# Three interleaved first groups instead of two, loaded and split in five parts, with eight warm-up matmuls instead of fourteen

## The chip, the cores and the metric

One NeuronCore of a Trainium2 chip runs the whole program. The metric is the device time of one execution in microseconds. TensorE (PE) multiplies, VectorE (DVE), ScalarE (ACT) and GpSimd (POOL) do elementwise work, and SyncE (SP) issues all the DMAs here. Each engine takes its own instructions in order; semaphores connect them.

## What is computed

x holds 64 sequences of 64 tokens with 1024 values each, so 4096 tokens. Four layers are applied one after another, each added to its input:

```python
x = x + _L0(x, lang, W, Wr, A, B)       # base x@W.T, plus top-2 gated low-rank experts (8 of rank 16)
x = x + _L1(x, cond, weights)           # a 64x64 matrix chosen per sequence, over the token axis
x = x + _L2(x, A[ids], B[ids])          # a rank-16 adapter chosen per sequence (64 adapters)
x = x + _L3(x, map, W, b, lA, lB)       # base x@W.T + b, plus a rank-16 adapter chosen per sequence (32)
```

## The kernel before, in words

All products are made in float32r with each operand split in a rounded high part and a low rest, in three passes (high x high, high x low, low x high). The split of a tile is an ACT instruction (the rounding, recorded at line 759) and then a DVE subtraction (line 1028).

**Weights first.** Up to about 300 us the kernel multiplies weights with weights, so that later every token tile needs fewer products: the matrices of the later layers are multiplied by (1 + W of layer 0), by the expert matrices and by the adapters. This is 61 groups. A group (list `GROUPS`, lines 56 to 58) is one stationary tile `stat` of 1024 x 128 (as 8 blocks of 128 x 128, 512 KB) times one chunk `mov` of 1024 x 512 (8 pieces of 128 x 512, 256 KB each): 8 steps k of 3 passes, so 24 matmuls of 512 columns into one PSUM bank (`product`, line 1390). The first nine groups share chunk 0 (`chunk_a`), the next nine chunk 1 (`chunk_b`).

**Stationary tiles** live in a ring of four slots (`RING`). `load_stat(g)` (line 379) waits until group g - 4 is done before it loads into that slot. For blocks of W of layer 0, POOL adds an identity to one block (line 655), which block depends on the group: blocks 4, 5 and 6 for groups 0, 1 and 2. Then ACT and DVE split the tile.

**The first groups.** Groups 0 and 1 run together (`TOGETHER`): for each k first the three passes of group 0, then of group 1 (lines 1397 to 1403), so that each piece of the chunk serves two groups as it arrives. Their tiles are loaded and split in two halves each, in the order half, piece 0, half, pieces 1 to 3, two halves, pieces 4 to 7 (lines 426 to 434 on SP, 822 to 830 on ACT, 1095 to 1103 on DVE). Tile 2 is loaded right behind, tile 3 at g = 0 of the loop.

**The loop over groups.** SP, ACT, DVE and POOL each run a loop over g of their own, written out by hand; its order is the order of each queue. In turn g, SP (lines 526 to 558) loads tile g + 3, then a piece of the next chunk, then 256 KB of `u3` rows (line 394), and stores the split u3 rows of the turn before (line 401), once they are split. ACT (lines 835 to 848) evicts group g - 1 (`group_hi`), rounds tile g + 2 (`stat_hi`), then a piece of the next chunk, then the u3 rows, which start at g = 1. DVE (lines 1133 to 1148) does the low parts in the same order. Before its loop DVE makes small setup tables (lines 1105 to 1127).

**Warm-up.** TensorE starts with 14 matmuls of the identity with itself (line 1385), which nobody reads.

**Token tiles.** From about 300 us on, 32 tiles of 128 tokens are processed in pairs. The change doesn't touch this.

Of the kernel before, what the change touches and what calls it, by code (L numbers as in the profile page):

```python
# [16 lines left out]
def build(nc, x, stat, mov, a0, wr, wc, u3, u2k, d3k, bias3, lang_ids, ids, out):  # L17
# [33 lines left out]

    TOGETHER, HALF_KB = 2, KB // 2
    M0_FIRST = M0_BLOCKS[HALF_KB:] + M0_BLOCKS[:HALF_KB]
# [31 lines left out]

    def halves(g, h):

        return h * TOGETHER + g + 1

# [65 lines left out]
    with ctx:  # L155
# [162 lines left out]
        def sem(name):  # L318
            return ctx.enter_context(nc.semaphore(name))

        ld_stat = [sem(f"ld_stat{n}") for n in range(RING)]
        ld_half = [[sem(f"ld_half{n}_{h}") for h in range(2)] for n in range(TOGETHER)]
        ld_mov = [[sem(f"ld_mov{n}_{k}") for k in range(KB)] for n in range(2)]
# [11 lines left out]
            sem, ("pool_const", "pool_stat", "pool_mov", "pool_md", "pool_mb", "pool_mix", "pool_s", "pool_ud"))  # L335
        act_half, act_stat, act_mov, act_u3, act_ev, act_hl, act_t = map(
            sem, ("act_half", "act_stat", "act_mov", "act_u3", "act_ev", "act_hl", "act_t"))
        act_x0, act_x1, act_s, act_part, act_ud, act_mix, act_exp = map(
            sem, ("act_x0", "act_x1", "act_s", "act_part", "act_ud", "act_mix", "act_exp"))
        act_h2, act_h2T, act_h3, act_h3T, act_hgT = map(sem, ("act_h2", "act_h2T", "act_h3", "act_h3T", "act_hgT"))  # L340
        act_yp, act_La, act_Lb, act_Ra, act_Rb = map(sem, ("act_yp", "act_La", "act_Lb", "act_Ra", "act_Rb"))
        dve_half, dve_stat, dve_mov, dve_u3, dve_ev, dve_hl, dve_set, dve_t1, dve_t4a, dve_t4, dve_t = map(
            sem, ("dve_half", "dve_stat", "dve_mov", "dve_u3", "dve_ev", "dve_hl", "dve_set", "dve_t1", "dve_t4a", "dve_t4",
                  "dve_t"))
# [31 lines left out]
        def _(sp):  # L376
# [44 lines left out]

            def load_half(g, h):
                own = slice(h * HALF_KB, (h + 1) * HALF_KB)
                sp.dma_start(sraw[g][:, own, :], stat[GROUPS[g][1]][:, own, :]).then_inc(ld_half[g][h], 16)

            load_half(0, 0)
            load_piece(0, 0)
            load_half(1, 0)
            for k in range(1, HALF_KB):
                load_piece(0, k)  # L430
            load_half(0, 1)
            load_half(1, 1)
            for k in range(HALF_KB, KB):
                load_piece(0, k)
            for g in range(TOGETHER, RING - 1):
# [199 lines left out]
        def _(pool):  # L635
# [11 lines left out]
            def stat_identity(g):  # L647
                s = GROUPS[g][1]
                if s in M0_BLOCKS:
                    raw = sraw[g % RING]  # L650
                    if g < TOGETHER:
                        pool.wait_ge(ld_half[g][s // HALF_KB], 16)
                    else:
                        pool.wait_ge(ld_stat[g % RING], 16 * slot_loads(g))
                    nc.gpsimd.tensor_tensor(out=raw[:, s, :], in0=raw[:, s, :], in1=ident[:, :], op=ALU.add).then_inc(pool_stat, 1)  # L655
# [101 lines left out]
        def _(act):  # L757
# [55 lines left out]

            def half_hi(g, h):
                own = slice(h * HALF_KB, (h + 1) * HALF_KB)
                if h == GROUPS[g][1] // HALF_KB:
                    act.wait_ge(pool_stat, stat_adds(g))
                else:
                    act.wait_ge(ld_half[g][h], 16)
                round_to(st[g][hi][:, own, :], sraw[g][:, own, :]).then_inc(act_half, 1)  # L820

            half_hi(0, 0)
            piece_hi(0, 0)
            half_hi(1, 0)
            for k in range(1, HALF_KB):
                piece_hi(0, k)
            half_hi(0, 1)
            half_hi(1, 1)
            for k in range(HALF_KB, KB):
                piece_hi(0, k)  # L830
            def x0_hi(j):
# [3 lines left out]
            for g in range(G):  # L835
                if g >= 1:
                    group_hi(g - 1)
                if g + 2 < G:
                    stat_hi(g + 2)
# [186 lines left out]
        def _(dve):  # L1026
# [62 lines left out]

            def half_lo(g, h):  # L1090
                own = slice(h * HALF_KB, (h + 1) * HALF_KB)
                dve.wait_ge(act_half, halves(g, h))
                rest(st[g][lo][:, own, :], sraw[g][:, own, :], st[g][hi][:, own, :]).then_inc(dve_half, 1)

            half_lo(0, 0)
            piece_lo(0, 0)
            half_lo(1, 0)
            for k in range(1, HALF_KB):
                piece_lo(0, k)
            half_lo(0, 1)  # L1100
            half_lo(1, 1)
            for k in range(HALF_KB, KB):
                piece_lo(0, k)

# [28 lines left out]
            for g in range(G):  # L1133
                if g >= 1:
                    group_lo(g - 1)
                if g + 2 < G:
                    stat_lo(g + 2)
# [246 lines left out]
        def _(pe):  # L1384
            WARM_UP = 14
            pe.wait_ge(pool_const, 2)
# [10 lines left out]
            for k in range(KB):  # L1397
                pe.wait_ge(dve_mov, k + 1)
                for g in range(TOGETHER):
                    pe.wait_ge(dve_half, halves(g, k // HALF_KB))  # L1400
                    last = product(g, k)
                    if k == KB - 1:
                        last.then_inc(pe_group, 1)
# [341 lines left out]
```

## Time and profile before

| | us |
|---|---|
| time, median of 3 runs | 910.5 (908.39 to 910.94) |
| profiled execution, device time | 909.23 |
| its span, first to last instruction | 907.5 |
| PE busy | 897.7 (99%) |
| DVE busy | 551.3 (61%) |
| ACT busy | 346.2 (38%) |
| POOL busy | 230.5 (25%) |
| DMA engines, mean busy share | 67% |

The span is what the profile covers; the device time of the same execution lies 1.7 us above it. A busy engine is one that is inside an instruction; a matmul's record covers its way through the array, so neighbours overlap and starts, not ends, tell the rate. Idle time of an engine that isn't the bottleneck costs nothing. The mean granted TensorE clock over the span is 0.998 of its full level.

### The profile page before, as it was taken

How to read it: one execution, taken by the hardware profiler on the slowest of the kernel's cores; microseconds unless marked ns; L12 is line 12 of the kernel's file. 1: busy time of each engine (PE TensorE's matmuls, PEld its weight loads, DVE VectorE, ACT ScalarE, POOL GpSimd, SP SyncE). 2: the span in 40 equal slices, each digit the busy share in tenths (PEclk: the TensorE clock that was granted, in tenths of full speed). 3: DMA queues.
4: the chain of work that ended last, by engine and by line, in shares of the span. 5: the costliest groups of instructions: out<-in, count | busy, mean ns of one | idle time of the engine just before them, and what ended most of it. 6: DMA issues, size and time to landing. Idle time of an engine off the chain costs nothing.

```text
span 907.5 us, 14863 instructions
## 1 busy us (share of the span) xinstructions
PE 897.7 (99%) x4788; PEld 798.2 (88%) x4788; DVE 551.3 (61%) x1421; ACT 346.2 (38%) x800; POOL 230.5 (25%) x349
## 2 busy tenths in 40 slices
PE   8999999999999999999999999999999999999997
PEld 7888888888888888999998998998998999999997
DVE  6554444354367426568567667577676576676675
ACT  5543343333334323333434433434434334334333
POOL 1010010011010003522523424414415325225230
PEclk9999999999999999999999999999999999999999
DMA  6878686999663563666756756766666567657664
GB/s 249 299 256 289 208 251 206 307 341 262 188 198 117 176 198 129 191 180 181 218 181 182 219 181 186 204 198 194 184 198 216 168 183 218 187 178 217 188 200 148
DMA packets 105602, 187.69 MB, mean 207 GB/s; under 512 B 15926, under 2 KB 66870, under 8 KB 105526
## 3 DMA queue, kind: packets, MB, share of 16 engines
q1 hardware_dynamic: 105526, 186.76, 66.9%
q8 instruction: 38, 0.62, 0.3%
q14 instruction: 38, 0.31, 0.1%
HBM read 143.20 MB, written 49.81 MB: 213 GB/s over the span
## 4 chain that ended last, share of the span: by engine, by line
PE 90%; SPq 4%; DMA 3%; issue 1%; POOL 1%; ACT 1%; DVE 0%; DVEq 0%; POOLq 0%
PE ps_o L1393 27%; PE ps_d L1419 16%; PE ps_w L1427 13%; PE ps_d L1427 9%; PE ps_s L1393 9%; PE ps_o L1440 5%; PE ps_d L1434 4%; PE ps_o L1451 3%; SPq L443 1%; PE ps_s L1457 1%; DMA mdraw<-t 1%; SPq L471 1%; PE ps_w L1434 1%; DMA mixraw<-wc 1%; DMA chunk_a_raw<-mov 1%
## 5 line engine op out<-in xcount | busy, mean ns | idle before, releaser
L1028 DVE TENSOR_TENSOR stat_lo<-stat_raw,stat_hi 128x1024 fp32r<-128x1024 f32 (+1 forms) x127 | 140.6, 1108 | 22.9 <-ACT stat_hi L759 20.4
L759 ACT ACTIVATE stat_hi<-stat_raw 128x1024 fp32r<-128x1024 f32 (+1 forms) x127 | 116.8, 932 | 17.1 <-POOL stat_raw L655 6.5
L1419 PE MATMUL ps_d<-w_hi,stat_hi 128*128 128x512 f32 x256 | 105.9, 414 | 0.8 <-POOL w_lo L680 0.8
L1419 PE MATMUL ps_d<-w_lo,stat_hi 128*128 128x512 f32 x256 | 101.1, 395 | 0.0
L1419 PE MATMUL ps_d<-w_hi,stat_lo 128*128 128x512 f32 x256 | 100.8, 394 | 0.0
L1393 PE MATMUL ps_o<-chunk_a_hi,stat_hi 128*128 128x512 f32 x216 | 84.5, 391 | 0.8 <-DVE chunk_a_lo L1028 0.7
L1393 PE MATMUL ps_o<-chunk_a_hi,stat_lo 128*128 128x512 f32 x216 | 84.1, 389 | 0.0
L1393 PE MATMUL ps_o<-chunk_a_lo,stat_hi 128*128 128x512 f32 x216 | 84.0, 389 | 0.0
L680 POOL CAST w_hi<-mdraw 128x512 fp32r<-128x512 f32 x32 | 20.0, 624 | 219.8 <-DMA mdraw<-t 219.8
L655 POOL TENSOR_TENSOR stat_raw<-stat_raw,ident 128x128 f32<-128x128 f32 x40 | 22.5, 562 | 184.9 <-DMA stat_raw<-stat 184.9
L1393 PE MATMUL ps_o<-chunk_b_hi,stat_hi 128*128 128x512 f32 x152 | 59.1, 389 | 0.0
L1393 PE MATMUL ps_o<-chunk_b_hi,stat_lo 128*128 128x512 f32 x152 | 59.1, 389 | 0.0
L1393 PE MATMUL ps_o<-chunk_b_lo,stat_hi 128*128 128x512 f32 x152 | 59.1, 389 | 0.0
L1419 PEld LDWEIGHTS ps_d<-w_hi,stat_hi 128*128 128x128 f32 x256 | 48.5, 190 | 10.8 <-issue 0.9
L1419 PEld LDWEIGHTS ps_d<-w_lo,stat_hi 128*128 128x128 f32 x256 | 48.1, 188 | 11.2
L1419 PEld LDWEIGHTS ps_d<-w_hi,stat_lo 128*128 128x128 f32 x256 | 48.4, 189 | 8.2
L759 ACT ACTIVATE y_hi<-y_raw 128x356 fp32r<-128x356 f32 x48 | 24.0, 499 | 66.9 <-DVE y_raw L1274 47.8
L1393 PEld LDWEIGHTS ps_o<-chunk_a_hi,stat_hi 128*128 128x128 f32 x216 | 40.5, 188 | 10.2 <-DVE chunk_a_lo L1028 1.4
L1245 DVE TENSOR_TENSOR outb<-ps_o,bias_row 128x356 f32<-128x356 f32 (+1 forms) x93 | 41.9, 506 | 10.7 <-PE ps_o L1451 10.3
L1393 PEld LDWEIGHTS ps_o<-chunk_a_lo,stat_hi 128*128 128x128 f32 x216 | 40.6, 188 | 8.4
L1393 PEld LDWEIGHTS ps_o<-chunk_a_hi,stat_lo 128*128 128x128 f32 x216 | 40.6, 188 | 8.3
L709 POOL TENSOR_TENSOR stat_raw<-stat_raw 128x512 f32<-128x512 f32 x32 | 44.5, 1390 | 12.7 <-DMA stat_raw<-x 11.1
(223 smaller groups left out, 2269.5 us busy)
## 6 DMA issues: line engine op xcount, KB each, us to landing
up<-tu SPq DMA_DIRECT2D x124, 256.0 KB, 4.2
stat_raw<-stat SPq DMA_DIRECT2D x59, 512.0 KB, 4.2
mdraw<-t SPq DMA_DIRECT2D x128, 208.0 KB, 2.9
stat_raw<-x SPq DMA_DIRECT2D x32, 512.0 KB, 3.5
out<-outb SPq DMA_DIRECT2D x30, 512.0 KB, 5.5
t<-md_a SPq DMA_DIRECT2D x16, 576.0 KB, 6.1
rows_raw<-x SPq DMA_DIRECT2D x32, 256.0 KB, 3.4
chunk_a_raw<-mov SPq DMA_DIRECT2D x24, 256.0 KB, 5.2
```

The source lines that it names most:

```text
L655: nc.gpsimd.tensor_tensor(out=raw[:, s, :], in0=raw[:, s, :], in1=ident[:, :], op=ALU.add).then_inc(pool_stat, 1)
L680: last = nc.gpsimd.tensor_copy(w[part][:, :, MD_AT:P_AT].rearrange("p k (q r) -> p k q r", r=RANK), rows.rearrange("p q (k r) -> p k q r", ...
L709: nc.gpsimd.tensor_tensor(out=dst, in0=in0, in1=in1, op=op).then_inc(pool_s, 1)
L759: return nc.scalar.activation(dst, src, ACT.Copy)
L1028: return nc.vector.tensor_tensor(out=dst, in0=src, in1=rounded.bitcast(F32), op=ALU.subtract)
L1245: nc.vector.tensor_tensor(out=dst[:, OX[n]], in0=out_bank(turn, n)[:, OK[n]], in1=bias_row[:, OX[n]], op=ALU.add).then_inc(dve_out[n], 1)
L1393: last = nc.tensor.matmul(ps_g[g % BANKS][:, :], st[g % RING][a][:, k, :], mchunk[c % 2][v][:, k, :], start=k == 0 and m == 0, stop=k == K ...
L1419: last = nc.tensor.matmul(plain_bank(t)[:, 0:WCOLS], rows[a][:, k, :], w[c][:, k, :], start=k == 0 and m == 0, stop=k == KB - 1 and m == l ...
L1427: last = nc.tensor.matmul(ps[:, 0:SH], rows[a][:, k, :], weights[c][:, k, :], start=first and k == 0 and m == 0, stop=k == HALF_KB - 1 and ...
L1434: last = nc.tensor.matmul(ps, hgT[t % 2][a][:, :], b03[c][:, cols], start=first and m == 0, stop=m == len(PASSES) - 1, skip_group_check=True)
L1440: last = nc.tensor.matmul(out_bank(turn, n)[:, 0:OW[n]], mix[turn % 2][a][:, :], y[t % 2][c][:, Y[n]], start=first and m == 0, stop=m == l ...
L1451: return nc.tensor.matmul(out_bank(turn, n)[:, OK[n]], stackT[:, :], up[:, OX[n]], start=first, stop=True, skip_group_check=True)
```

## The change

The first three groups run together instead of two. Their tiles are no longer loaded and split in two halves of four blocks, but in five parts of 1, 1, 2, 2 and 2 blocks. For each part SP loads the part of all three tiles, then the pieces of the chunk with the same k. One semaphore a part (`ld_part[q]`) counts all three tiles' loads, and whoever uses any of them waits for all three. ACT and DVE take tile 0's part, the first piece, the parts of tiles 1 and 2, and then the second piece, if there is one. Tile 3 is loaded in the loop's first turn, as before, and its split stands right behind the parts, on DVE ahead of the setup tables. Warm-up has 8 matmuls. The diff, without the renamed semaphores:

```diff
@@ -49,7 +49,8 @@
     M0_BLOCKS, B0_BLOCK, U2_BLOCKS = list(range(KB)), KB, list(range(KB + 1, 2 * KB + 1))
     D_CHUNKS, M3_CHUNKS = (0, 1, 2), (3, 4)
 
-    TOGETHER, HALF_KB = 2, KB // 2
+    TOGETHER, HALF_KB = 3, KB // 2
+    PARTS = (range(0, 1), range(1, 2), range(2, 4), range(4, 6), range(6, 8))
     M0_FIRST = M0_BLOCKS[HALF_KB:] + M0_BLOCKS[:HALF_KB]
 
     M0_BY_TWO = [s + h for s in range(HALF_KB) for h in (0, HALF_KB)]
@@ -83,9 +84,12 @@
 
         return g // RING + (1 if g % RING >= TOGETHER else 0)
 
-    def halves(g, h):
-
-        return h * TOGETHER + g + 1
+    def parts(g, q):
+
+        return q * TOGETHER + g + 1
+
+    def part_of(k):
+        return [k in ks for ks in PARTS].index(True)
 
     def piece(c, k):
         return c * KB + k
...
@@ -419,19 +423,15 @@
                 sp.dma_start(table[first:first + OWN, :, RAW_AT:FULL].bitcast(F32),
                              source[first:first + OWN].rearrange("a p k r -> a p (k r)")).then_inc(st_own, 16)
 
-            def load_half(g, h):
-                own = slice(h * HALF_KB, (h + 1) * HALF_KB)
-                sp.dma_start(sraw[g][:, own, :], stat[GROUPS[g][1]][:, own, :]).then_inc(ld_half[g][h], 16)
-
-            load_half(0, 0)
-            load_piece(0, 0)
-            load_half(1, 0)
-            for k in range(1, HALF_KB):
-                load_piece(0, k)
-            load_half(0, 1)
-            load_half(1, 1)
-            for k in range(HALF_KB, KB):
-                load_piece(0, k)
+            def load_part(g, q):
+                own = slice(PARTS[q].start, PARTS[q].stop)
+                sp.dma_start(sraw[g][:, own, :], stat[GROUPS[g][1]][:, own, :]).then_inc(ld_part[q], 16)
+
+            for q, ks in enumerate(PARTS):
+                for g in range(TOGETHER):
+                    load_part(g, q)
+                for k in ks:
+                    load_piece(0, k)
             for g in range(TOGETHER, RING - 1):
                 load_stat(g)
             sp.dma_start(lang_sb[:, :], lang_ids[None, :].to_broadcast([P, TILES * BT])).then_inc(ld_lang, 16)
@@ -649,7 +649,7 @@
                 if s in M0_BLOCKS:
                     raw = sraw[g % RING]
                     if g < TOGETHER:
-                        pool.wait_ge(ld_half[g][s // HALF_KB], 16)
+                        pool.wait_ge(ld_part[part_of(s)], 16 * TOGETHER)
                     else:
                         pool.wait_ge(ld_stat[g % RING], 16 * slot_loads(g))
                     nc.gpsimd.tensor_tensor(out=raw[:, s, :], in0=raw[:, s, :], in1=ident[:, :], op=ALU.add).then_inc(pool_stat, 1)
@@ -811,23 +811,23 @@
                     last = round_to(both[hi][:, n, :], raw[:, n, :])
                 last.then_inc(act_t, 1)
 
-            def half_hi(g, h):
-                own = slice(h * HALF_KB, (h + 1) * HALF_KB)
-                if h == GROUPS[g][1] // HALF_KB:
+            def part_hi(g, q):
+                own = slice(PARTS[q].start, PARTS[q].stop)
+                if GROUPS[g][1] in PARTS[q]:
                     act.wait_ge(pool_stat, stat_adds(g))
                 else:
-                    act.wait_ge(ld_half[g][h], 16)
-                round_to(st[g][hi][:, own, :], sraw[g][:, own, :]).then_inc(act_half, 1)
-
-            half_hi(0, 0)
-            piece_hi(0, 0)
-            half_hi(1, 0)
-            for k in range(1, HALF_KB):
-                piece_hi(0, k)
-            half_hi(0, 1)
-            half_hi(1, 1)
-            for k in range(HALF_KB, KB):
-                piece_hi(0, k)
+                    act.wait_ge(ld_part[q], 16 * TOGETHER)
+                round_to(st[g][hi][:, own, :], sraw[g][:, own, :]).then_inc(act_part0, 1)
+
+            for q, ks in enumerate(PARTS):
+                part_hi(0, q)
+                piece_hi(0, ks[0])
+                for g in range(1, TOGETHER):
+                    part_hi(g, q)
+                for k in ks[1:]:
+                    piece_hi(0, k)
+            stat_hi(TOGETHER)
+
             def x0_hi(j):
                 act.wait_ge(ld_x0, 16 * (j + 1))
                 round_to(x0[hi][:, :, :], x0raw[:, :, :]).then_inc(act_x0, 1)
@@ -835,7 +835,7 @@
             for g in range(G):
                 if g >= 1:
                     group_hi(g - 1)
-                if g + 2 < G:
+                if TOGETHER < g + 2 < G:
                     stat_hi(g + 2)
                 for c, k in pieces_at(g):
                     piece_hi(c, k)
@@ -1087,20 +1087,19 @@
                     last = rest(both[lo][:, n, :], raw[:, n, :], both[hi][:, n, :])
                 last.then_inc(dve_t, 1)
 
-            def half_lo(g, h):
-                own = slice(h * HALF_KB, (h + 1) * HALF_KB)
-                dve.wait_ge(act_half, halves(g, h))
-                rest(st[g][lo][:, own, :], sraw[g][:, own, :], st[g][hi][:, own, :]).then_inc(dve_half, 1)
-
-            half_lo(0, 0)
-            piece_lo(0, 0)
-            half_lo(1, 0)
-            for k in range(1, HALF_KB):
-                piece_lo(0, k)
-            half_lo(0, 1)
-            half_lo(1, 1)
-            for k in range(HALF_KB, KB):
-                piece_lo(0, k)
+            def part_lo(g, q):
+                own = slice(PARTS[q].start, PARTS[q].stop)
+                dve.wait_ge(act_part0, parts(g, q))
+                rest(st[g][lo][:, own, :], sraw[g][:, own, :], st[g][hi][:, own, :]).then_inc(dve_part0, 1)
+
+            for q, ks in enumerate(PARTS):
+                part_lo(0, q)
+                piece_lo(0, ks[0])
+                for g in range(1, TOGETHER):
+                    part_lo(g, q)
+                for k in ks[1:]:
+                    piece_lo(0, k)
+            stat_lo(TOGETHER)
 
             dve.wait_ge(ld_lang, 16)
             dve.wait_ge(pool_const, CONSTS)
@@ -1133,7 +1132,7 @@
             for g in range(G):
                 if g >= 1:
                     group_lo(g - 1)
-                if g + 2 < G:
+                if TOGETHER < g + 2 < G:
                     stat_lo(g + 2)
                 for c, k in pieces_at(g):
                     piece_lo(c, k)
@@ -1382,7 +1381,7 @@
 
         @block.tensor
         def _(pe):
-            WARM_UP = 14
+            WARM_UP = 8
             pe.wait_ge(pool_const, 2)
             for _ in range(WARM_UP):
                 nc.tensor.matmul(ps_w[:, 0:P], ident[:, :], ident[:, :], start=True, stop=True)
@@ -1397,7 +1396,7 @@
             for k in range(KB):
                 pe.wait_ge(dve_mov, k + 1)
                 for g in range(TOGETHER):
-                    pe.wait_ge(dve_half, halves(g, k // HALF_KB))
+                    pe.wait_ge(dve_part0, parts(g, part_of(k)))
                     last = product(g, k)
                     if k == KB - 1:
                         last.then_inc(pe_group, 1)
```

## Rows read from the trace of the kernel before

**Rows 1.** The page: busy us of each engine, share of the span.
```profile
PE 897.7 (99%) x4788; PEld 798.2 (88%) x4788; DVE 551.3 (61%) x1421; ACT 346.2 (38%) x800; POOL 230.5 (25%) x349
```

**Rows 2.** Stretches: length; busy us of PE, PEld, DVE, ACT, POOL; clock, DMA, GB/s.
```profile
0.00:20.00 20.00, 17.72 (x78) 14.88 (x79) 11.95 (x25) 11.02 (x17) 3.61 (x14) 1.00 0.67 241
```

**Rows 3.** Waits up to 80 us: engine, line <- releaser: us, times, longest.
```profile
PEld ps_o L1393 <- DVE chunk_a_lo L1028: 1.4, 2, 1.2
```

**Rows 4.** Timeline to 7.3 us: start, us, engine, line, what [idle before].
```profile
0.75 0.40 SPq L424 DMA_DIRECT2D stat_raw<-stat  x1
1.21 0.42 SPq L388 DMA_DIRECT2D chunk_a_raw<-mov  x1
1.53 5.93 PE L1388 MATMUL ps_w<-ident 128*128 128x128 f32 x28 [1.53 <-POOL ident L638]
...
4.44 0.63 ACT L759 ACTIVATE chunk_a_hi<-chunk_a_raw 128x512 fp32r<-128x512 f32 x1
...
5.75 0.69 DVE L1028 TENSOR_TENSOR stat_lo<-stat_raw,stat_hi 128x512 fp32r<-128x512 f32 x1
7.22 0.47 PE L1393 MATMUL ps_o<-chunk_a_hi,stat_hi 128*128 128x512 f32 x1
```

**Rows 5.** Timeline, 8 to 20 us: the chunk's pieces and group 2.
```profile
8.16 1.89 ACT L759 ACTIVATE chunk_a_hi<-chunk_a_raw 128x512 fp32r<-128x512 f32 x3 [2.44 <-DMA chunk_a_raw<-mov]
...
9.57 0.50 PE L1393 MATMUL ps_o<-chunk_a_hi,stat_hi 128*128 128x512 f32 x1 [0.72 <-DVE chunk_a_lo L1028]
...
18.24 1.22 DVE L1028 TENSOR_TENSOR stat_lo<-stat_raw,stat_hi 128x1024 fp32r<-128x1024 f32 x1
...
19.52 0.50 PE L1393 MATMUL ps_o<-chunk_a_hi,stat_hi 128*128 128x512 f32 x1
```

**Rows 6.** Timeline of TensorE: first matmuls of group 3 and of group 4.
```profile
25.13 0.39 PE L1393 MATMUL ps_s<-chunk_a_hi,stat_hi 128*128 128x512 f32 x1
...
30.57 0.39 PE L1393 MATMUL ps_o<-chunk_a_hi,stat_hi 128*128 128x512 f32 x1
```

**Rows 7.** L1388 alone: one stretch; grouped by form, 5.5:6.2 and 6.9:7.2 us.
```profile
1.53:6.88 5.35, 5.35 (x25) 5.35 (x26) 1.00 0.77 242
...
L1388 PE MATMUL ps_w<-ident 128*128 128x128 f32 x6 | 1.5, 421 | 0.0
...
L1388 PE MATMUL ps_w<-ident 128*128 128x128 f32 x5 | 0.9, 310 | 0.0
```

**Rows 8.** Groups by line and form, whole span: a 128x128 tile on DVE.
```profile
L1176 DVE TENSOR_TENSOR hg<-ps_d,gates 128x128 f32<-128x128 f32 x32 | 9.3, 291 | 1.1
```

**Rows 9.** Table of stretches, 4 to 12 us, columns as in rows 2.
```profile
4.00:8.00 4.00, 4.00 (x23) 3.88 (x22) 2.01 (x3) 1.66 (x3) 0.00 (x0) 1.00 0.74 240
8.00:12.00 4.00, 3.28 (x15) 2.38 (x14) 2.16 (x4) 2.74 (x5) 1.33 (x2) 1.00 1.05 407
```

**Rows 10.** Timeline: group 0's last matmul, SP's load into slot 0, first u3 rows.
```profile
18.42 0.39 PE L1393 MATMUL ps_o<-chunk_a_lo,stat_hi 128*128 128x512 f32 x1
...
18.84 0.33 SPq L383 DMA_DIRECT2D stat_raw<-stat  x1
...
19.68 0.43 SPq L394 DMA_DIRECT2D rows_raw<-u  x1
```

**Rows 11.** Timeline, 22 to 29 us: what happens to tile 4.
```profile
22.41 0.46 POOL L655 TENSOR_TENSOR stat_raw<-stat_raw,ident 128x128 f32<-128x128 f32 x1 [5.11 <-DMA stat_raw<-stat]
...
25.46 0.63 ACT L759 ACTIVATE rows_hi<-rows_raw 128x512 fp32r<-128x512 f32 x1 [4.55 <-DMA rows_raw<-u]
...
26.48 1.05 ACT L759 ACTIVATE stat_hi<-stat_raw 128x1024 fp32r<-128x1024 f32 x1
...
27.56 1.23 DVE L1028 TENSOR_TENSOR stat_lo<-stat_raw,stat_hi 128x1024 fp32r<-128x1024 f32 x1
```

**Rows 12.** The u3 loads (L394), all eight: time from issue to landing.
```profile
DMA to landing us min/median/max: 3.4/3.7/6.8
```

**Rows 13.** Timeline of DVE: low part of tile 5.
```profile
30.51 1.22 DVE L1028 TENSOR_TENSOR stat_lo<-stat_raw,stat_hi 128x1024 fp32r<-128x1024 f32 x1
```

More of the change, by code:

```diff
@@ L321, in build @@
         ld_stat = [sem(f"ld_stat{n}") for n in range(RING)]
-        ld_half = [[sem(f"ld_half{n}_{h}") for h in range(2)] for n in range(TOGETHER)]
+        ld_part = [sem(f"ld_part{q}") for q in range(len(PARTS))]
         ld_mov = [[sem(f"ld_mov{n}_{k}") for k in range(KB)] for n in range(2)]
@@ L335, in build @@
             sem, ("pool_const", "pool_stat", "pool_mov", "pool_md", "pool_mb", "pool_mix", "pool_s", "pool_ud"))
-        act_half, act_stat, act_mov, act_u3, act_ev, act_hl, act_t = map(
-            sem, ("act_half", "act_stat", "act_mov", "act_u3", "act_ev", "act_hl", "act_t"))
+        act_part0, act_stat, act_mov, act_u3, act_ev, act_hl, act_t = map(
+            sem, ("act_part0", "act_stat", "act_mov", "act_u3", "act_ev", "act_hl", "act_t"))
         act_x0, act_x1, act_s, act_part, act_ud, act_mix, act_exp = map(
@@ L341, in build @@
         act_yp, act_La, act_Lb, act_Ra, act_Rb = map(sem, ("act_yp", "act_La", "act_Lb", "act_Ra", "act_Rb"))
-        dve_half, dve_stat, dve_mov, dve_u3, dve_ev, dve_hl, dve_set, dve_t1, dve_t4a, dve_t4, dve_t = map(
-            sem, ("dve_half", "dve_stat", "dve_mov", "dve_u3", "dve_ev", "dve_hl", "dve_set", "dve_t1", "dve_t4a", "dve_t4",
+        dve_part0, dve_stat, dve_mov, dve_u3, dve_ev, dve_hl, dve_set, dve_t1, dve_t4a, dve_t4, dve_t = map(
+            sem, ("dve_part0", "dve_stat", "dve_mov", "dve_u3", "dve_ev", "dve_hl", "dve_set", "dve_t1", "dve_t4a", "dve_t4",
                   "dve_t"))
```

## The prediction

> **What bounds the kernel now.** The page first: TensorE is busy 897.7 us, 99% of the span [rows 1], so only what makes TensorE wait can move the time, and the change touches it only in the first groups. The table of stretches says how much there is to win: of the first 20 us TensorE was busy 17.72 [rows 2]. So about 2.3 us of idle time, 1.53 of it before the first warm-up matmul, plus whatever the warm-up matmuls themselves cover. The waits name most of the rest: the weight loads of TensorE stood 1.4 us behind pieces of the moving chunk [rows 3]. The timeline gives the places. Warm-up runs from 1.53, the first real matmul starts at 7.22, although its operands were split by about 6.4 (the last entry of DVE is 5.75 + 0.69): here warm-up itself is late [rows 4]. After six matmuls TensorE idles until 9.57, because piece 1 landed only at 8.16, and group 2 starts at 19.52 behind a split that DVE began at 18.24, after its setup work [rows 5]. Group 3 starts at 25.13 and group 4 at 30.57; these are 24 matmuls or 5.44 us apart, so 0.2267 us a matmul, without a gap [rows 6].
>
> **Part 1, warm-up.** TensorE made 25 records in the 5.35 us from 1.53 to 6.88, 0.214 us each [rows 7]; a warm-up matmul leaves two (28 for 14). Eight make 16 x 0.214 = 3.4 us and end near 5.0. The clock matters: in the last stretch before the first real matmul the same instruction shortened from 421 ns to a mean of 310 ns [rows 7], so TensorE went from its lower level (1.2 GHz) to its upper (2.4 GHz) near 6.9, after 5.35 us of unbroken work. After the change it works 3.4 us, pauses until the first operands are there, and goes on. Either the rise comes as early as now (cost nothing) or, at the worst the rows allow, after another 5.35 us of unbroken work. No row decides.
>
> The Trainium skill, page "TensorE: Matmul & The Clock Gate", Part 1, says that the engine begins throttled and that activity releases it. The trace agrees in kind; what a pause in warm-up does no row here shows.
>
> **Part 2, the loads.** Now four halves and eight pieces, 12 loads of 256 KB. After: 15 parts (six of 64 KB, nine of 128 KB) and eight pieces, 23 loads, 3.5 MB instead of 3 MB. SP starts one each 0.46 us [rows 4]. Piece 0 moves from second to fourth, its issue from 1.21 to 0.75 + 3 x 0.46 = 2.13. It now lands 3.2 us after its issue at the latest (ACT takes it at 4.44) [rows 4]; I take 3.1, so 5.2. Then 0.63 on ACT and 0.69 on DVE [rows 4] make 6.55, and the first matmul starts at 6.6, not 7.22. The small parts cost 0.29 us each on DVE [rows 8], and not more on ACT, which was the shorter of the two at 512 columns; they fit between. Nine matmuls take 2.04 us, to 8.65. Piece 1 is the eighth load, issued at 3.97, with 896 KB up to and with it. Bounds for its landing: 3.97 + 3.2 = 7.2 and the 8.13 of now (1024 KB) [rows 5]. I take 7.7, since the same slow stretch of 4 to 8 us (240 GB/s) lies across it [rows 9]; with ACT and DVE it is ready at 9.1, a stall of 0.45. From then a step of 448 KB is wanted each 2.04 us, 220 GB/s, while 407 arrived from 8 to 12 us [rows 9], and DVE needs 0.69 + 3 x 0.29 = 1.6 us a step: no further stall. The three identity adds on POOL (0.5 us) lie ahead of steps 4 to 7, some 2 us before they are needed. Group 2's late split disappears too, as it is now part of these. Seven steps: 9.1 + 14.3 = 23.4 is where group 3 can start, against 25.13: a gain of 1.75 us. Tile 3's load moves back behind 11 more issues on SP, to about 14 us, and has 9 us to land and be split; nothing.
>
> With the clock at its lower level until 6.6 + 5.35 = 11.95, matmuls come each 0.43 us: 12.5 of 72 by then, the other 59.5 take 13.5, and group 3 starts at 25.4. I take half of this 2.0 us, since the pause is short beside the work around it: 24.4.
>
> The Trainium skill, page "DMA: Bandwidth & Descriptors", section Bandwidth, speaks against this part: it wants transfers batched to 1 MiB and gives a 64 KB one 138 GB/s. By that rate, an estimate, the six small loads (393 KB) would take 2.8 us of the engines, and the time would be some 1.5 us higher than mine. The rows have no load of such a size in this stretch.
>
> **Part 3, what comes free later.** This is the edit's other side. The ring has four slots; group 4's tile goes into slot 0, and SP waits for group 0's end to load it. Now group 0's last matmul is the 45th of 48; SP issues at 18.84, and its companions follow: a piece, then u3 rows at 19.68 [rows 10]. What follows is a chain in which ACT's order counts: group 0's eviction, then the u3 rows (landed 25.46), group 1's eviction, and only then tile 4 at 26.48, although it had landed by 22.41; DVE splits it from 27.56 to 28.79 [rows 11]. So from SP's issue to "tile 4 ready" it takes 9.95 us, and group 4 starts at 30.57 [rows 6]: a slack of only 1.8 us. With three groups interleaved, group 0's last matmul is the 66th of 72. It starts 7 x 0.2267 = 1.59 before group 3, and SP issues 0.42 after (now 18.42 and 18.84 [rows 10]). With 24.4 that is 23.2, 4.4 us later than now. Queued behind SP's wait are a piece of chunk b, the u3 rows and group 5's tile, as now, so the chain moves as a block. Its length is bounded from below by the rows landing in the median 3.7 us instead of 5.8 (7.9 us in all) and from above by their longest, 6.8 (11.0) [rows 12]. I take 9.3, nearer to the one measured in the same burst of loads. Group 4 then starts at 32.5 instead of 24.4 + 5.44 = 29.8: TensorE stalls 2.7 us, and against 30.57 the kernel is 1.95 us later. Tile 5 was ready at 31.73 [rows 13], 12.9 after SP's issue, so 36.1, and is wanted at 32.5 + 5.44 = 37.9; tile 6 follows a whole group later with its load. The delay of group 4 passes unchanged to the end, as TensorE is saturated there.
>
> **Sum.** Group 3 starts now 16.3 us of matmuls and 1.6 of stalls after 7.22. After: start -0.6, stalls 0.45 for 1.6 -1.15, clock +1.0, so 0.75 earlier; then the stall in front of group 4, +2.7; net +1.95. The profiled execution took 909.23 us with a span of 907.5, so 911.2 for it; it lies 1.3 under the median of 910.5, which gives 912.4.
>
> **Rivals.** (a) The change does what it seems to be for: the clock rises in time and the u3 rows land in 3.7 us. Group 3 at 23.4, SP at 22.2, tile 4 at 30.1, so 0.5 us earlier than now; with tile 4 earlier still, TensorE's own 23.4 + 5.44 = 28.85 and 1.7 us. 908.8 to 910.0. For it: at least half of the eight loads of u3 rows landed within 3.7 us [rows 12]. Against: the one that counts took 5.8, in a burst of six loads after an idle stretch, as it will again. Chance 0.22. (b) Slower: the clock. The pause between warm-up and work keeps TensorE at the lower level to about 12 us. Group 3 at 25.4, SP at 24.2, tile 4 at 34.2: +3.6, 914.1. It decides once the rise comes later than about 10 us. For it: the unbroken 5.35 us of now. Chance 0.2. (c) Small loads are slow, so that piece 1 lands 1.5 us later; everything follows, +3.4, 913.9. Chance 0.08. The forecast itself, tile 4's chain with the clock somewhere between, has 0.5, and its own range is +0.7 to +2.7: 911.2 to 913.2.
>
> **Chances.** About 0.3%, or 2.7 us, is what a measurement can tell from no change. Faster by more than that wants (a) beyond its end and a lucky spread of runs: 0.08. Slower by more is (b), and the larger part of (c): 0.24. Within: 0.68. The range takes in (a)'s upper part and (b): 909.0 to 914.3.
>
> **What would show it.** Right: SP's load into slot 0 near 22 to 23.5, TensorE idle in front of group 4 for 2 to 3 us with DVE's split of tile 4 as what ended it, group 3 starting before 25. Wrong: group 4 starting before 30.57, u3 rows landing in under 4 us, no idle time in front of group 4. The clock's step: L1393 matmuls 0.43 us apart after 6.9. Should a second stall stand before group 5 or 6, or group 3 start late because of tile 3, the sum is short of a term.

## The result, and the profile after

The changed kernel took 912.52 us (median of 22 runs), the kernel before 910.56 us beside it: a ratio of 1.0029, 95% interval 1.0016 to 1.0042. The medians lie 2.0 us apart, the means (913.43 and 910.69) 2.7, since the changed kernel has some long executions, up to 919.61. By the ratio it is slower by 1.5 to 3.8 us, about 2.6 us, just under the 0.3% that the prediction named as what can be told from no change. The forecast was 912.4.

The page of the changed kernel, first line of busy times, answers to [rows 1]. Then TensorE's waits, which name what is new, and the stretches (length, then busy us of PE, PEld, DVE, ACT, POOL, then clock, DMA share, GB/s).

```profile
PE 897.3 (99%) x4776; PEld 797.6 (88%) x4776; DVE 548.3 (60%) x1431; ACT 348.3 (38%) x810; POOL 232.5 (26%) x349
```
```profile
PE ps_o L1450 <- ACT h2T L759: 2.5, 3, 1.9
PE ps_o L1392 <- DVE stat_lo L1028: 2.2, 1, 2.2
PE ps_w L1387 <- POOL ident L638: 1.5, 1, 1.5
PE ps_o L1392 <- DVE chunk_a_lo L1028: 1.1, 1, 1.1
```
```profile
0.00:40.00 40.00, 35.19 (x146) 29.02 (x146) 22.34 (x47) 19.90 (x39) 5.11 (x17) 1.00 0.74 242
40.00:300.00 260.00, 260.00 (x1149) 215.29 (x1148) 131.64 (x182) 100.42 (x162) 26.16 (x48) 1.00 0.78 241
```

TensorE has as much work as before, fewer by the twelve warm-up records. A wait of 2.2 us behind `stat_lo` is new. From 40 to 300 us nothing waits, and the same 1149 matmul records stand there before and after, so all that the weight part loses is lost in the first 40.

The timeline of its start, start time first, then duration (answers to [rows 4] and [rows 5]):

```profile
1.53 3.78 PE L1387 MATMUL ps_w<-ident 128*128 128x128 f32 x16 [1.53 <-POOL ident L638]
...
2.14 0.43 SPq L392 DMA_DIRECT2D chunk_a_raw<-mov  x1
...
6.36 0.80 PE L1392 MATMUL ps_o<-chunk_a_hi,stat_hi 128*128 128x512 f32 x1 [1.05 <-DVE chunk_a_lo L1028]
...
7.38 0.63 PE L1392 MATMUL ps_o<-chunk_a_lo,stat_hi 128*128 128x512 f32 x1
...
7.61 0.63 ACT L759 ACTIVATE chunk_a_hi<-chunk_a_raw 128x512 fp32r<-128x512 f32 x1 [0.39 <-DMA chunk_a_raw<-mov]
7.81 0.63 PE L1392 MATMUL ps_o<-chunk_a_hi,stat_hi 128*128 128x512 f32 x1
...
10.25 0.39 PE L1392 MATMUL ps_o<-chunk_a_hi,stat_hi 128*128 128x512 f32 x1
```

Warm-up is over early, and the first real matmul starts at 6.36 instead of 7.22. But it has a record of 0.80 us, and the seven behind it stand 0.43 us apart and last 0.63 us, not 0.39: TensorE was at 1.2 GHz until 10.1, where its clock record says that it rose. The chain that ended last shows the rest, start and length:

```profile
6.36 17.01 PE ps_o L1392 x66
23.37 0.02 issue
23.39 0.33 SPq L387
...
24.23 4.63 DMA rows_raw<-u
28.86 0.02 issue
28.89 0.64 ACT rows_hi L759
29.52 0.49 ACT md_a L759
30.01 0.95 ACT stat_hi L759
30.96 0.02 issue
30.98 1.36 DVE stat_lo L1028
32.34 0.04 issue
32.38 16.62 PE ps_o L1392 x72
```

This is the chain of the forecast, link by link: 66 matmuls to group 0's end, SP's load into slot 0 (which lets the u3 rows behind it go), the u3 rows' landing, their rounding, an eviction, tile 4's rounding, its low part, group 4. Tile 4 itself had been there before: POOL began its addition at 27.44, 2.6 us before ACT took the tile up at 30.01. Group 3 starts at 24.55 (before 25.13), group 4 at 32.38 (before 30.57 [rows 6]).

```profile
24.55 0.39 PE L1392 MATMUL ps_s<-chunk_a_hi,stat_hi 128*128 128x512 f32 x1
...
27.44 0.46 POOL L655 TENSOR_TENSOR stat_raw<-stat_raw,ident 128x128 f32<-128x128 f32 x1 [8.24 <-DMA stat_raw<-stat]
```

So 0.6 us won at group 3 became 1.8 us lost at group 4.

### The profile page after: what moved, and what is told of

Its sections match the earlier page's. It is cut to its first block, busy times and chain, and to the rows that moved or that the text cites. A ratio compares the mean times of both kernels' runs of the same rounds, so it can differ in the third digit from the quotient of the medians.

```text
span 910.2 us, 14869 instructions
## 1 busy us (share of the span) xinstructions
PE 897.3 (99%) x4776; PEld 797.6 (88%) x4776; DVE 548.3 (60%) x1431; ACT 348.3 (38%) x810; POOL 232.5 (26%) x349
## 4 chain that ended last, share of the span: by engine, by line
PE 89%; DMA 3%; SPq 3%; issue 1%; POOL 1%; ACT 1%; DVE 1%; DVEq 0%; POOLq 0%
PE ps_o L1392 27%; PE ps_d L1418 17%; PE ps_w L1426 12%; PE ps_d L1426 9%; PE ps_s L1392 8%; PE ps_o L1439 4%; PE ps_d L1433 4%; PE ps_o L1450 3%; DMA mdraw<-t 2%; PE ps_s L1456 1%; SPq L443 1%; PE ps_w L1433 1%; DMA stat_raw<-x 1%; SPq L456 1%; DMA rows_raw<-u 1%
## 5 line engine op out<-in xcount | busy, mean ns | idle before, releaser
L1028 DVE TENSOR_TENSOR stat_lo<-stat_raw,stat_hi 128x1024 fp32r<-128x1024 f32 (+3 forms) x137 | 143.6, 1051 | 28.0 <-ACT stat_hi L759 25.5
L759 ACT ACTIVATE stat_hi<-stat_raw 128x1024 fp32r<-128x1024 f32 (+3 forms) x137 | 118.5, 880 | 22.4 <-POOL stat_raw L655 8.9
```

Source lines behind the costliest of these rows:

```text
L759: return nc.scalar.activation(dst, src, ACT.Copy)
L1028: return nc.vector.tensor_tensor(out=dst, in0=src, in1=rounded.bitcast(F32), op=ALU.subtract)
```

## Experiments

Two theories stood against each other for the main loss. The first: ACT takes the u3 rows ahead of tile 4, and with slot 0 free 4.5 us later this wait ends last. The rival: slot 0 is simply free too late, whatever ACT does. A second question was what the short warm-up does to TensorE's clock. In these profiled executions I read four points: when TensorE's clock rose (from the granted clock, which agrees with the length of the matmuls), when groups 3 and 4 started, and the time from SP's load into slot 0 to tile 4's low part done (the chain). The single executions of a kernel scatter over several us (those of the kernel before, beside the changed one, from 907.85 to 913.54), so that the times need their intervals, and one profiled execution stands for itself only. Ratios are to the kernel before in the same batch, since that kernel's own median moved from 908.5 to 910.7 us between batches.

### 14 warm-up matmuls in the changed kernel

```diff
-            WARM_UP = 8
+            WARM_UP = 14
```

> The changed kernel with 14 warm-up matmuls instead of 8, all else as changed. Theory (the pause after a short warm-up delays TensorE's clock): the clock rises near 7 us instead of 10.1, no L1392 matmul stands 0.43 us from the next, group 3 starts near 23.6 instead of 24.55, SP loads slot 0 near 22.4, group 4 starts near 31.4 instead of 32.4; the time is about 1.0 us under that of the changed kernel and about 1 us over the kernel before. Rival (the clock rises when it does, whatever warm-up does, and the later start of real work at 7.2 costs what it saved): group 3 at 24.5 or later, group 4 at 32.4 or later, no gain.

Measured: 912.86 us beside 908.51 of the kernel before, ratio 1.0052 (1.0031 to 1.0073). The clock rose at 6.3, and group 3 started at 23.80, 0.75 us earlier: so far the theory. SP loaded slot 0 at 22.64. But the u3 rows landed only at 29.5, and group 4 started at 32.89, after a longer stall:

```profile
29.52 0.63 ACT L759 ACTIVATE rows_hi<-rows_raw 128x512 fp32r<-128x512 f32 x1 [5.75 <-DMA rows_raw<-u]
...
31.61 1.23 DVE L1028 TENSOR_TENSOR stat_lo<-stat_raw,stat_hi 128x1024 fp32r<-128x1024 f32 x1
...
32.89 0.50 PE L1392 MATMUL ps_o<-chunk_a_hi,stat_hi 128*128 128x512 f32 x1 [3.48 <-DVE stat_lo L1028]
```

And something that I had not foreseen. The stretches behind the stall (clock is the third number from the end):

```profile
25.00:33.60 8.60, 5.12 (x23) 3.94 (x22) 4.06 (x7) 3.82 (x7) 0.92 (x2) 1.00 0.78 257
33.60:37.00 3.40, 3.40 (x10) 2.63 (x9) 2.77 (x4) 1.34 (x2) 0.46 (x1) 0.50 0.95 321
37.00:40.00 3.00, 3.00 (x14) 2.47 (x14) 1.42 (x3) 2.23 (x4) 0.00 (x0) 1.00 1.02 365
```

The granted clock fell to one half at 33.6 and came back at 37.0. The (x10) counts every matmul that touches the stretch; TensorE started 8 in these 3.4 us, 0.43 us apart, where it starts 15 at 0.2267, so that the fall cost some 7 x 0.2267 = 1.6 us on top of the stall's 3.5. SP's load was 0.75 us earlier, but the chain behind it took 10.2 us instead of 8.9, since the rows landed in 6.0 us and not in 4.7; the head start went into a longer stall. That the time would fall with group 3 is not borne out: 1.0 us less than the changed kernel was expected, and by the ratios it is 2.1 us more.

### The u3 rows two turns later in the changed kernel

```diff
-    U3_FIRST, U3_UNITS = 1, 2 * NE3 * RANK // P
+    U3_FIRST, U3_UNITS = 3, 2 * NE3 * RANK // P
```

> The changed kernel with the u3 rows loaded and split from turn 3 on instead of turn 1, so that ACT does not stand behind their landing before it rounds tiles 4 and 5. Theory (the stall before group 4 is ACT's order: u3 rows ahead of tile 4): tile 4 is rounded as soon as it has landed, some 4 us after SP's issue, and is ready 6.9 us after the issue instead of 8.9; group 4 starts near 30.3 instead of 32.4, and the time falls 2.1 us, to that of the kernel before or slightly under. Rival (slot 0 free too late: the load itself and the two splits make the stall): tile 4's load lands no earlier, group 4 starts at 32 or later, the time stays. Second rival: the rows come in the way of a later tile (a stall in front of group 6 to 8), so that the time is given back.

Measured: 908.16 us, ratio to the kernel before 0.9995 (0.9979 to 1.0011), where the changed kernel has 1.0029. Nothing waits in front of group 4, which starts at 29.90, its 24 matmuls after group 3 at 24.46. SP's load went out at 23.29, no earlier than in the changed kernel, and the chain took 6.2 us, not 8.9:

```profile
26.64 0.46 POOL L655 TENSOR_TENSOR stat_raw<-stat_raw,ident 128x128 f32<-128x128 f32 x1 [7.53 <-DMA stat_raw<-stat]
27.13 1.06 ACT L759 ACTIVATE stat_hi<-stat_raw 128x1024 fp32r<-128x1024 f32 x1 [2.23 <-POOL stat_raw L655]
...
28.23 1.22 DVE L1028 TENSOR_TENSOR stat_lo<-stat_raw,stat_hi 128x1024 fp32r<-128x1024 f32 x1 [2.06 <-ACT stat_hi L759]
```

The stall is gone with slot 0 free as late as ever, so the rival falls. No later tile stalled. By the ratios the gain over the changed kernel is 3.1 us, more than the 2.1 expected; the section on the hardware has what may be the rest.

### Two groups together in five parts, 8 warm-up matmuls

```diff
-    TOGETHER, HALF_KB = 3, KB // 2
+    TOGETHER, HALF_KB = 2, KB // 2
```

> The changed kernel with two groups together instead of three, still in five parts and with 8 warm-up matmuls. Theory (the third interleaved group is what delays slot 0): group 0 ends near 19, SP loads slot 0 near 19, tile 4 is ready near 28.5 to 29 and nothing stalls in front of group 4; group 3 starts at 24.5 to 25.0, group 4 at 30 to 30.5; the time is 1.5 to 2.4 us under the changed kernel, so from equal to 0.6 us under the kernel before. Rival (parts and short warm-up are what costs): group 4 starts at 31.5 or later even so.

Measured: 909.82 us, ratio 1.0014 (0.9997 to 1.0030). Slot 0 was loaded at 18.68, tile 4 ready at 28.9, group 3 started at 24.61 and group 4 at 30.05 without a stall, although the clock rose only at 10.7:

```profile
18.68 0.33 SPq L387 DMA_DIRECT2D stat_raw<-stat  x1
...
27.67 1.22 DVE L1028 TENSOR_TENSOR stat_lo<-stat_raw,stat_hi 128x1024 fp32r<-128x1024 f32 x1
...
30.05 0.39 PE L1392 MATMUL ps_o<-chunk_a_hi,stat_hi 128*128 128x512 f32 x1
```

The third group is what turned the slack of 1.8 us into a stall; the five parts don't. The time missed its range (from equal to 0.6 us under the kernel before): the median lies 1.3 us over it, and its interval overlaps that of the changed kernel, so that it is the trace that tells the two apart here, not the time. The third group with the old halves was not run.

### 8 warm-up matmuls in the kernel before

```diff
-            WARM_UP = 14
+            WARM_UP = 8
```

> The kernel before with 8 warm-up matmuls instead of 14. Theory (a pause in TensorE's work delays its clock): first real matmul near 6.5 instead of 7.2, clock rising near 10 instead of 6.9; its six matmuls take 2.6 us instead of 1.4 and piece 1 is late anyway, so little is lost at first; group 2 starts 0 to 0.6 us later than 19.5, group 4 0 to 0.6 us later than 30.6, time +0 to +0.6. Rival (the clock does not care): group 2 at 19.5 as now, time equal, clock at 6.9.

Measured: 908.36 us, ratio 0.9997 (0.9978 to 1.0015), so no difference that can be measured. The one profiled execution is the extreme of all: first matmul at 5.91, but the clock at its lower level until 13.95, 4 us later than expected, and groups 3 and 4 at 26.60 and 32.04, 1.5 us behind the kernel before.

```profile
5.91 0.79 PE L1393 MATMUL ps_o<-chunk_a_hi,stat_hi 128*128 128x512 f32 x1 [0.59 <-DVE chunk_a_lo L1028]
...
9.37 0.80 PE L1393 MATMUL ps_o<-chunk_a_hi,stat_hi 128*128 128x512 f32 x1 [0.54 <-DVE chunk_a_lo L1028]
...
13.38 0.63 PE L1393 MATMUL ps_o<-chunk_a_hi,stat_hi 128*128 128x512 f32 x1
...
14.33 0.39 PE L1393 MATMUL ps_o<-chunk_a_hi,stat_hi 128*128 128x512 f32 x1
```

TensorE paused twice here, 0.6 us before the first matmul and 0.5 us before the seventh. The expected range for group 4 was missed by 0.9 us, since I had taken 10 us as the latest rise. The median doesn't move with it, and the profiled execution (910.45 us) lies 2.1 us over the median, so other executions probably had an earlier rise. That this kernel has one is not shown; the split order below, with 8 warm-up matmuls too, shows two.

### 14 warm-up matmuls and late u3 rows

```diff
-            WARM_UP = 8
+            WARM_UP = 14
-    U3_FIRST, U3_UNITS = 1, 2 * NE3 * RANK // P
+    U3_FIRST, U3_UNITS = 3, 2 * NE3 * RANK // P
```

> The changed kernel with 14 warm-up matmuls and with the u3 rows from turn 3 on. Theory (two separate costs, the late clock and the u3 rows ahead of tile 4 on ACT): clock up near 6.3 to 6.9, group 3 near 23.8 as with 14 warm-up matmuls alone, tile 4 ready some 7 us after SP's issue at 22.6, so group 4 starts near 29.3 to 29.6 and TensorE idles under 0.6 us in front of it; the clock does not fall. Time 0.4 to 0.9 us under the kernel with late u3 rows and 8 warm-up matmuls, 1 us under the kernel before. Rival (warm-up length does nothing for the sum): group 4 starts at 29.9 or later, as with 8.

Measured: 910.81 us, ratio 1.0015 (0.9998 to 1.0032). The expected gain did not come. The clock rose at 6.8 and never fell, and nothing stalled in front of group 4, but group 3 started only at 24.40 and group 4 at 29.84, as with 8. The full clock ran TensorE into the pieces, at 12.0, as its waits show:

```profile
PE ps_o L1392 <- DVE chunk_a_lo L1028: 0.5, 1, 0.5
```

So what the rival said of the sum holds here: 14 warm-up matmuls brought group 4 nothing, and the ratio is 0.0020 (1.8 us) over that of late u3 rows with 8, where 0.4 to 0.9 us less was expected.

### The u3 rows split one turn later

SP loads them as in the changed kernel; only the order of ACT and DVE changes.

```diff
-                for u in u3_at(g):
+                for u in u3_at(g - 1):
                     u3_hi(u)
...
-                for u in u3_at(g):
+                for u in u3_at(g - 1):
                     u3_lo(u)
```

> The changed kernel with the u3 rows loaded by SP exactly where they are, but split by ACT and DVE one turn later, behind tile 4's split. It tells ACT's order from the transfer itself. Theory (the order on ACT): tile 4 is rounded as soon as it has landed and POOL has added, near 27.5 to 28.5, is ready near 30.3, and group 4 starts near 30.3 instead of 32.4; time 2 us under the changed kernel. Rival (the u3 load takes bandwidth from tile 4 and the late u3 case gained from its absence): tile 4 lands 4 us or more after SP's issue and group 4 starts at 31.5 or later, or a later tile stalls because SP stands in front of the rows' store.

Measured: 908.44 us, ratio 0.9983 (0.9967 to 1.0000). SP's load at 23.89, tile 4 rounded as soon as it was there, ahead of the u3 rows:

```profile
27.45 0.46 POOL L655 TENSOR_TENSOR stat_raw<-stat_raw,ident 128x128 f32<-128x128 f32 x1 [7.79 <-DMA stat_raw<-stat]
27.94 1.06 ACT L759 ACTIVATE stat_hi<-stat_raw 128x1024 fp32r<-128x1024 f32 x1 [2.44 <-POOL stat_raw L655]
...
29.86 0.63 ACT L759 ACTIVATE rows_hi<-rows_raw 128x512 fp32r<-128x512 f32 x1 [0.34 <-DMA rows_raw<-u]
```

The u3 rows took 5.1 us to land (24.74 to 29.86) and held up nobody. The chain took 6.4 us, and group 4 followed group 3 (25.06) without a gap, at 30.50. It is the order on ACT, not the transfer. By the ratios the time is 4.2 us under the changed kernel, twice the 2 us expected. In this execution the clock rose early, at 4.5, inside warm-up; the first real matmul at 6.55 was fast at once, and TensorE then waited 1.0 us at 12.6 for a piece. The early clock bought nothing either.

### Two groups in five parts, 14 warm-up matmuls

```diff
-    TOGETHER, HALF_KB = 3, KB // 2
+    TOGETHER, HALF_KB = 2, KB // 2
-            WARM_UP = 8
+            WARM_UP = 14
```

> The changed kernel with two groups together and 14 warm-up matmuls: the five parts alone are left of the change. Theory: the clock is up by 6.9, the first real matmul starts at 7.2, step 1 is ready at 8.2 to 8.9, group 3 starts at 23.9 to 24.4 and group 4 at 29.3 to 29.9 without a stall (slot 0 free near 18.3, tile 4 ready near 28.3); time 0.7 to 1.2 us under the kernel before. Rival (the parts cost as much as they bring): group 4 starts at 30.5 or later.

Measured: 909.99 us, ratio 1.0005 (0.9986 to 1.0024). Clock at 7.3, group 3 at 24.70, group 4 at 30.14, no stall: 0.4 us ahead of the kernel before at group 4, where 0.7 to 1.3 was expected, and not to be seen in the time. Parts alone bring little.

### Late u3 rows in the kernel before

```diff
-    U3_FIRST, U3_UNITS = 1, 2 * NE3 * RANK // P
+    U3_FIRST, U3_UNITS = 3, 2 * NE3 * RANK // P
```

> The kernel before with the u3 rows from turn 3 on: the control for the late u3 rows. Theory: there is no stall before group 4 to remove (1.8 us of slack), so group 4 starts at 30.6 as before and the time is the same within what can be measured; tile 4 is ready 2 us earlier, near 26.8. Rival (late u3 rows help anywhere, by less traffic early): group 3 or 4 starts over 0.5 us earlier, time 0.5 us or more lower.

Measured: 909.28 us, ratio 0.9992 (0.9978 to 1.0006). DVE began tile 4's low part at 24.22 instead of 27.56, and group 4 started at 30.29, 0.3 us earlier, as group 3 did. Tile 4 was ready 5 us before it was needed, and it brought nothing: with slack there is nothing to win from the order. This is the control for late u3 rows and for the split order.

### The changed kernel again, beside the split order

> The changed kernel itself once more, beside the two below on the same chip. Theory: tile 4 stands behind the u3 rows on ACT, so group 4 starts 8.9 to 10.3 us after SP's load into slot 0, with a stall of 2 to 3.5 us in front of it, and the time is 2 to 3 us over the kernel before. The clock rises anywhere from 4.5 to 14 us, since with 8 warm-up matmuls it has risen at 4.5, 10.0, 10.1, 10.7 and 14.0. Rival: the stall seen in one execution was its own, and this one shows none.

Measured: 913.26 us, ratio 1.0030 (1.0011 to 1.0049), a stall of 3.1 us in front of group 4 at 33.21. The clock rose at 9.9 and fell behind this stall too:

```profile
33.21 0.50 PE L1392 MATMUL ps_o<-chunk_a_hi,stat_hi 128*128 128x512 f32 x1 [3.06 <-DVE stat_lo L1028]
...
33.80:37.20 3.40, 3.40 (x10) 2.66 (x9) 2.90 (x4) 1.25 (x2) 0.45 (x1) 0.50 0.90 304
37.20:40.00 2.80, 2.80 (x14) 2.27 (x13) 1.14 (x2) 1.81 (x3) 0.00 (x0) 1.00 1.04 363
```

The split order again, same edit as above:

> The changed kernel with the u3 rows split one turn later, again, beside the changed kernel. Theory: no stall in front of group 4, ready 6.4 to 7 us after SP's load; time 2 to 3 us under the changed kernel and 1 to 1.5 us under the kernel before. Rival: the lead over the kernel before was chance; then it is within 0.5 us of it.

Measured: 909.54 us, ratio 0.9987 (0.9971 to 1.0003); so 3.7 us under the changed kernel, more than the stall and than the 2 to 3 us expected, and 1.1 us under the kernel before, a lead that its interval doesn't tell from nothing. The chain took 6.9 us, group 4 started at 29.85 with a wait of 0.2 us, the clock had risen at 5.1.

And with 14 warm-up matmuls:

```diff
-            WARM_UP = 8
+            WARM_UP = 14
```

> The changed kernel with the u3 rows split one turn later and 14 warm-up matmuls. Theory: the clock rises by 7.3 at the latest, first real matmul at 7.0 to 7.4, group 3 at 23.6 to 24.4, group 4 at 29.1 to 29.9, no stall; time equal to the 8 warm-up case within 0.7 us, since an early rise there buys back a late one. Rival (the clock is the larger cost): 1 us or more under the 8 warm-up case.

Measured: 910.25 us, ratio 0.9988 (0.9967 to 1.0009). Clock at 6.5, group 3 at 24.52, group 4 at 30.23, both 0.1 to 0.3 us later than the latest expected. The time is that with 8 within 0.7 us, as the theory said.

All profiled executions together, in us; the chain runs from SP's load into slot 0 to tile 4's low part done:

| kernel | clock up | group 3 | chain | stall | group 4 | ratio to before |
|---|---|---|---|---|---|---|
| before | 6.9 | 25.13 | 9.95 | none | 30.57 | 1 |
| before, 8 warm-up | 14.0 | 26.60 | 11.1 | none | 32.04 | 0.9997 |
| before, u3 rows late | 7.2 | 24.85 | 6.9 | none | 30.29 | 0.9992 |
| two groups in parts | 10.7 | 24.61 | 10.2 | none | 30.05 | 1.0014 |
| two groups in parts, 14 | 7.3 | 24.70 | 9.5 | none | 30.14 | 1.0005 |
| changed | 10.1 | 24.55 | 8.9 | 2.2 | 32.38 | 1.0029 |
| changed, again | 9.9 | 24.55 | 9.8 | 3.1 | 33.21 | 1.0030 |
| changed, 14 | 6.3 | 23.80 | 10.2 | 3.5 | 32.89 | 1.0052 |
| u3 rows late | 10.0 | 24.46 | 6.2 | none | 29.90 | 0.9995 |
| u3 rows late, 14 | 6.8 | 24.40 | 6.5 | none | 29.84 | 1.0015 |
| split order | 4.5 | 25.06 | 6.4 | none | 30.50 | 0.9983 |
| split order, again | 5.1 | 24.07 | 6.9 | 0.2 | 29.85 | 0.9987 |
| split order, 14 | 6.5 | 24.52 | 6.8 | none | 30.23 | 0.9988 |

## Why the prediction was right

**What bounds.** TensorE, and only the first 40 us: right. In the later part the changed kernel's execution lost another 0.9 us (877.8 us from group 4 to the end, against 876.9), with more waiting for `h2T` among the token tiles (2.5 us, before 1.2). Other executions took from 875.1 to 880.9 there, the longest being one of the kernel before with late u3 rows; I take it for scatter, which no term of the sum stood for.

**Part 1, warm-up.** The worst case was a rise at 11.95, the best no change, and I took half of the 2.0 us between. It rose at 10.1. That a short warm-up can bring a late rise was right: it was late, 9.9 or later, in five of the seven executions with 8 matmuls and in none of the six with 14. But half the worst case stands for no single execution: in two of the seven the clock was up at 4.5 and 5.1, before warm-up ended, so that 10.1 was one draw of several. And the price was too high. The price hung on group 3 starting at 23.4 with a full clock, and no execution reached this: with the clock up by 7.3, the three-group kernels started it at 23.80, 24.40, 24.52, 25.06 and 24.07, a mean of 24.4, and with a late clock at 24.55, 24.46 and 24.55. So a rise near 10 cost 0.2 us, not 1.0, as far as executions whose pieces landed differently can tell; two groups in parts agree (24.61 with the rise at 10.7, 24.70 at 7.3). A rise at 14 did cost: 1.5 us at group 3, in the kernel before with 8. The bound of 11.95 was wrong too: the kernel before with 8 warm-up matmuls rose at 13.95. "Unbroken work" does not hold as a rule on the other side either, as it rose at 4.5 after 3 us of work.

**Part 2, the loads.** First matmul at 6.36 (6.6 expected), piece 1 on ACT at 7.61 (7.7). The step that failed is "no further stall", which put that term at nothing: at full clock TensorE caught up with the pieces, with waits of 0.5 to 1.0 us near 12 us in four of the five executions named above. In the changed kernel the low clock hid them: piece 2's low part was done at 11.56 (DVE from 10.87), and TensorE came to it only at 12.31. The two errors, a price of 1.0 us for the clock alone and none for the pieces, cancelled: group 3 at 24.55 for 24.4. That is luck. The small loads did not show the price that the Trainium skill, page "DMA: Bandwidth & Descriptors", would give them: by 138 GB/s I had estimated 1.5 us more, and the first matmul came 0.2 us and piece 1 0.1 us ahead of the sum.

**Part 3, what comes free later.** Right in mechanism and size: SP's load at 23.39 (23.2), chain 8.9 us (9.3), group 4 at 32.38 (32.5), 1.8 us later than before (1.95). The u3 rows were there 4.7 us after their issue, between the bounds, and the late rows and the split order show that ACT's order makes the stall. Tile 5 was in time, as expected. Missing is the clock's fall behind the stall: it fell in two of three executions with a stall, those of 3.1 and 3.5 us, not in that of 2.2, and cost 1.6 us each time. The forecast used an idle TensorE as if it cost only its idle time. The profiled execution took 912.17 us where the sum gave 911.2, with 1.8 of the 2.9 us explained by the sum, 0.9 lost behind group 4 and 0.2 outside the span. Over all executions the ratio says 2.6 us, 0.8 more than that 1.8; the fallen clock can account for it, as the last section works out. That the median came out within 0.2 us of 912.4 is partly luck.

**Rivals.** (a), the gain, did not occur: the u3 rows took 4.7 us or more wherever ACT waited for them first. (b) was to decide once the rise came later than about 10 us. It came at 10.1, and group 3 started at 24.55, not at 25.4: (b) priced the clock at the start, and the clock's cost came at the stall instead. (c) wanted piece 1 to land 1.5 us later than 7.7; ACT had it at 7.61.

## What to carry to other kernels

Interleaving more groups over a ring of buffers makes the first buffer free later, by all the extra groups' work: count from the last use of each slot, not from the first. Where an engine works through a handwritten order, look for what stands ahead of the tile that is needed next, and put what nobody waits for behind it; here this turned a loss of 0.3% into equal or slightly better (0.9983 and 0.9987, with intervals that end at 1.0000 and 1.0003). And starting a saturated engine earlier is worth nothing if the next buffer isn't earlier too: even without the stall the third group put group 4 at 29.84 to 30.50, where two groups in the same parts had it at 30.05 and 30.14.

## What the runs showed of the hardware

**TensorE's clock can fall behind a stall.** The stalls of 3.1 and 3.5 us were each followed, 0.6 to 0.7 us after work had begun again, by 3.4 us at a granted clock of 0.50, at 1.6 us each. The stall of 2.2 us was not, and in the ten executions without such a stall the clock never fell between its rise and 904 us, near the end. The Trainium skill, page "TensorE: Matmul & The Clock Gate", Part 1, says that activity releases the throttle and idle time brings it back; the trace agrees for two of the three stalls, with the fall only once work had resumed.

**How often it falls can be read without a profile.** Every execution has its mean granted clock on record, and one such fall, 3.4 us at one half, lowers it by about 0.002. The eleven profiled executions without a fall have 0.998 or more. At 0.997 or less are 27 of the 43 executions of the three runs whose kernels stalled (the changed kernel twice, and with 14 warm-up matmuls), 6 of the 60 of late u3 rows and split order in the changed kernel, 8 of 96 of the kernel before beside the experiments, and 8 of 46 of the other four kernels, 5 of these with two groups in parts and 14 warm-up matmuls. In the changed kernel's two runs the executions at 0.997 or less took 1.4 and 1.6 us longer on average than its others, the price of one fall. So the clock probably costs the changed kernel about 1 us on average, on top of the 1.8 us at group 4. This is an estimate: where in an execution the clock was low, only the profiled ones show.

**When it rises at the start is not fixed by the kernel.** With 14 warm-up matmuls it rose between 6.3 and 7.3 in six executions. With 8 it rose at 4.5, 5.1, 9.9, 10.0, 10.1, 10.7 and 14.0 in seven. The long warm-up made the rise steady, but gained no time that could be measured: in the five pairs of kernels that differ in it alone, the ratio with 14 and with 8 is 1 and 0.9997, 1.0052 and 1.0029, 1.0015 and 0.9995, 1.0005 and 1.0014, 0.9988 and 0.9987. In the four three-group executions in which TensorE waited near 12 us, it waited for pieces that weren't there any earlier.

**Landing depends on the burst.** The first u3 rows, 256 KB behind 768 KB of other loads after an idle queue, took 4.7 to 6.9 us from issue to use in the ten executions that load them in turn 1 (4.7, 5.1, 5.3, 5.5, 5.6, 5.8, 6.0, 6.0, 6.1, 6.9), where the median landing time of all eight such loads in the kernel before is 3.7 [rows 12]. The cost to plan with is that of the same place in the same kind of burst.
